# Audio tower on one core: expert heads rotated over the column tiles of TensorE, expert mixing in one 32x32 step, pooling weights moved into the stationary operand, gate logits as a product

## Chip, cores and metric

One core of a Trainium2 chip runs the whole kernel. The metric is the device time of one execution in microseconds. The kernel before takes 988.88 us (median of 3 runs, 986.07 to 990.84).

## What is computed

Every value is fp32. The reference, cut to what matters here:

```
h = tok(x, w, b)                       # x: 128 batches x 64 features x 750 times
h = h + attn(layernorm(h), Q, K, VO)
h = h + ffn(layernorm(h), ...)         # h: 128 batches x 94 tokens x 64 features

tok:    windows of 8 times; scores = x.w + b; weights = softmax over the 8;
        pooled = sum(x * weights)      # -> 94 tokens
attn:   8 heads of rank 32; softmax(q k^T / 8) over all 94 tokens; ctx = attn @ x;
        out = sum over heads of ctx @ VO
ffn:    4 heads n of width 16: sx = x @ hl_w + hl_b
        4 experts e per head: q_e = sx wq_e, k = sx wk, v = sx wv
        att = softmax(4 q k^T + causal); qkv = att v; qkv = 0 where sx == 0
        gs = softmax over e of (gate_w . qkv + gate_b); mixed = sum_e qkv_e gs_e
        hn = layernorm(mixed + resid); two 16x16 layers with relu; layernorm -> fout
        fg = softmax over the 4 heads of fout @ fgate_w^T
        out = fout * fg
```

## The kernel before

Four batches make a **quad**; there are 32. Tokens are padded to 96 and cut into three blocks of 32, called j = 0, 1, 2; nearly every tile has the 128 partitions (batch b, token within the block), with j, head and expert in the free dimension. A quad passes through some ten stages: scores of the pooling softmax (`tok_score`), transposes of x (`turn`), pooling (`pool_x`), first layer norm, attention (`project`, `score`, `exp_s`, `norm_p`, `turn_p`, `mix`, `give_outT`, `give_out`), second layer norm, the experts' projections (`front_...`), their scores (`score3`), softmax (`soft` on VectorE, the exponential on ScalarE in `exp_p3` after a transpose `turn_p3`), mixing with v (`mix3`), the mask (`guard`), the transpose back with the gate's product (`turn_c`), the gate, a norm, two small layers (`layer1`, `layer2`), a norm, the head gate and the store.

The whole is a software pipeline written out by hand. Each engine has a function `quad` that is run once per iteration and lists the steps in a fixed order, each for a different quad (`g - 3`, `g - 4`, ...); an iteration of the loop does one whole quad's worth of each step. The engines run their lists strictly in order and wait for each other by semaphores. The eight PSUM banks are shared by fixed numbers that stand in the calls, so a step on TensorE also waits until VectorE or ScalarE has emptied its bank. No scheduler is at work: the lists and the bank numbers are the schedule.

Three kinds of fact about the code matter below.

- A matmul occupies a **tile** of the 128x128 array: contraction rows x columns of its stationary operand, in multiples of 32. The profile prints it in front of the shape, as `64*32`. Matmuls on different tiles of one shape may run side by side. An fp32 matmul is executed as two passes, so the profile counts two instructions for one of the code; transposes are one each.
- `mix3` works in three shapes: `96*32` for token block 2 (L793), `32*32` for block 0 (L797, head n on rows 32n and columns 32n, so four of the sixteen tiles are used), `64*32` for block 1 (L801). To bring v onto the partitions that this needs, SyncE's queue copies it with four DMAs per quad (`move_v`).
- `scale_x` multiplies x in PSUM by the softmax weights of the pooling on VectorE, four instructions per quad (L1348, L1353); `pool_x` then sums with a constant 0/1 matrix `pick` as the stationary operand. The head gate is a product of `fo` with the broadcast `wfg` on GpSimd (L529) and a sum on VectorE (L1517).

## Time and profile before

| | |
|---|---|
| time, median of 3 runs | 988.88 us (986.07 to 990.84) |
| the profiled execution | 985.96 us, span 984.0 us |
| TensorE busy | 903.5 us, 92% |
| VectorE busy | 815.4 us, 83% |
| ScalarE busy | 732.6 us, 74% |
| GpSimd busy | 719.0 us, 73% |
| TensorE clock, mean over the span | 0.967 of full |
| DMA moved | 36.48 MB, mean 37 GB/s |

Read it as an average over three parts: a filling part in which only the first stages have work, some 28 iterations that all look alike, and an emptying part. Only windows inside the middle part tell what an iteration costs.

### The profile page before, as it was taken

To read this page: it belongs to the slowest core of one execution; us is meant where nothing else is said; L and a number is where in the kernel's file an instruction comes from. 1 tells how busy PE (TensorE), PEld (TensorE's weight loads), DVE (VectorE), ACT (ScalarE), POOL (GpSimd) and SP (SyncE) were. 2 spreads that over 40 slices of the span, in tenths; PEclk is the share of its full clock that TensorE was granted. 3 is DMA by queue.
4 is the path that set the end of the run, shared out by engine and by line. 5 is a ranking of instruction groups with operands and counts; after the bars stand their busy time and mean duration, and the time that the engine had idled before them with its cause. 6 is when DMAs were issued, how large, how long until landed. Compare 5 with 4: busy or idle time off the path is not lost.

```text
span 984.0 us, 39626 instructions
## 1 busy us (share of the span) xinstructions
PE 903.5 (92%) x16320; PEld 604.0 (61%) x16320; DVE 815.4 (83%) x1916; ACT 732.6 (74%) x2759; POOL 719.0 (73%) x1055
## 2 busy tenths in 40 slices
PE   4798999999999999999999999999999999989841
PEld 3365666666666666666666666666666666656630
DVE  3545687889898888989899888989899888889877
ACT  1566878878888888878878888878888888885520
POOL 2333245577888787888888787878889788879893
PEclk9778999999999999999999999999999999999975
DMA  6301111110111011111111011111100000000000
GB/s 199 105 7 35 42 42 41 41 42 10 45 45 36 15 43 45 45 45 45 45 45 42 11 43 44 44 46 45 45 14 14 7 13 11 14 13 15 17 8 17
DMA packets 40931, 36.48 MB, mean 37 GB/s; under 512 B 27312, under 2 KB 30512, under 8 KB 40752
## 3 DMA queue, kind: packets, MB, share of 16 engines
q1 hardware_dynamic: 40406, 33.91, 12.3%
q8 instruction: 129, 2.11, 0.9%
q14 instruction: 50, 0.41, 0.1%
q10 hardware_dynamic: 250, 0.05, 0.0%
q0 software_dynamic: 96, 0.00, 0.0%
HBM read 25.08 MB, written 3.08 MB: 29 GB/s over the span
## 4 chain that ended last, share of the span: by engine, by line
PE 75%; ACT 16%; DVE 6%; issue 1%; DMA 1%; POOL 1%; POOLq 0%; DVEq 0%
ACT pu L1123 14%; PE psum L782 10%; PE psum L808 9%; PE psum L703 7%; PE psum L731 6%; PE psum L693 5%; PE psum L685 5%; PE psum L767 5%; PE psum L610 4%; PE psum L635 3%; PE psum L711 3%; PE psum L801 2%; PE psum L821 2%; PE psum L797 2%; PE psum L817 2%; PE psum L621 2%
## 5 line engine op out<-in xcount | busy, mean ns | idle before, releaser
L1123 ACT ACTIVATE pu<-psum,mx 128x94 f32<-128x94 f32 x768 | 248.2, 370 | 8.0 <-DVE mx L1404 6.7
L1123 ACT ACTIVATION_READ_ACCUMULATOR pu<-psum,mx 128x1 f32 x768 | 182.2, 238 | 0.0
L474 POOL TENSOR_TENSOR pu<-pu,pr 128x752 f32<-128x752 f32 x96 | 138.6, 1446 | 34.3 <-DVE pr L1408 34.2
L1404 DVE TENSOR_REDUCE mx<-psum 128x8 f32<-128x752 f32 x96 | 90.1, 939 | 87.3 <-PE psum L693 83.1
L1166 ACT ACTIVATE pT<-psum 96x512 f32<-96x512 f32 (+1 forms) x224 | 131.1, 601 | 34.1 <-PE psum L782 29.9
L508 POOL TENSOR_TENSOR st<-st,neg_half 128x12 f32<-128x12 f32 x64 | 146.0, 2281 | 5.0
L782 PE MATMUL psum<-ident_w,pu 128*96 128x128 f32 (+1 forms) x896 | 132.1, 277 | 13.2 <-ACT pu L1123 7.4
L1433 DVE TENSOR_REDUCE mx<-psum 128x16 f32<-128x1536 f32 (+2 forms) x96 | 116.5, 1213 | 11.2 <-PE psum L767 11.2
L782 PEld LDWEIGHTS psum<-ident_w,pu 128*96 128x96 f32 (+1 forms) x896 | 99.5, 135 | 39.8 <-issue 17.2
L1436 DVE TENSOR_TENSOR pu<-psum,mx 128x1536 f32<-128x1536 f32 (+2 forms) x96 | 117.5, 1224 | 3.3
L808 PE MATMUL psum<-gx,ct 128*128 128x84 f32 x768 | 101.9, 276 | 0.0
L808 PEld LDWEIGHTS psum<-gx,ct 128*128 128x128 f32 x768 | 93.9, 193 | 12.9 <-issue 12.9
L693 PE MATMUL psum<-kp,xT 64*32 64x376 f32 x1536 | 83.4, 491 | 8.4 <-ACT pu L1123 6.4
L1412 DVE STREAM_TRANSPOSE pT<-pu 128x768 f32<-128x768 f32 x96 | 87.6, 941 | 0.0
L731 PE MATMUL psum<-x3T,aq 64*128 64x384 f32 x256 | 78.9, 522 | 0.0
L1128 ACT ACTIVATE cT<-psum 128x384 f32<-128x384 f32 x128 | 53.9, 493 | 33.5 <-PE psum L703 33.4
L1170 ACT ACTIVATE oc<-psum 128x336 f32<-128x336 f32 x96 | 43.0, 448 | 47.8 <-PE psum L808 47.8
L703 PE MATMUL psum<-pT,xn 32*64 32x384 f32 x1536 | 70.1, 489 | 0.3 <-ACT kp L1151 0.3
L1116 ACT ACTIVATE kp<-psum 128x384 f32<-128x384 f32 x128 | 59.7, 500 | 13.3 <-PE psum L685 13.3
L767 PE MATMUL psum<-kp,sxT 32*32 32x256 f32 (+2 forms) x3072 | 69.1, 389 | 0.0
L1444 DVE SCALAR_TENSOR_TENSOR ct<-sxT,psum 128x512 f32<-128x512 f32 x96 | 65.4, 681 | 4.1 <-PE psum L801 1.9
L525 POOL TENSOR_TENSOR ft<-ft,fx 128x192 f32<-128x192 f32 x29 | 17.2, 592 | 70.0 <-DVE ft L1512 70.0
(187 smaller groups left out, 2203.2 us busy)
## 6 DMA issues: line engine op xcount, KB each, us to landing
xs<-in_x SPq DMA_DIRECT2D x64, 375.0 KB, 3.7
vb<-va SPq DMA_DIRECT2D x32, 128.0 KB, 2.2
out_h<-ho SPq DMA_DIRECT2D x126, 16.0 KB, 1.4
out_h<-ho SPq DMA_DIRECT2D x126, 7.5 KB, 1.4
vc<-va SPq DMA_DIRECT2D x96, 16.0 KB, 2.2
gx<-in_L_ffn_gate_w SPq DMA_DIRECT2D x16, 0.2 KB
fc<-in_L_ffn_fc_w SPq DMA_DIRECT2D x12, 1.0 KB
fc<-in_L_ffn_fc_b SPq DMA_DIRECT2D x12, 0.1 KB
```

Of the source, the lines that this page charges most:

```text
L474: pool.tensor_tensor(p, p, bcast(pr[:, j, :, :].rearrange("p a b -> p (a b)"), 2, NTOK), ALU.mult).then_inc(at_normed, 1)
L508: pool.tensor_tensor(st[:, k, 3, :], st[:, k, 2, :], neg_half[:, 0:NJ * NH], ALU.pow).then_inc(rstd, 1)
L693: mm = pe.matmul(psum[TB * b:TB * b + TB, (low, high)[par], 0:HP * NTOK], xT[rows, p, b, TB * j:TB * j + TB], kp[rows, p, b, :, 0:NTOK], s ...
L703: mm = pe.matmul(psum[64 * par:64 * par + 64, banks[b], 0:HP * TP], xn[rows, r, ub, 0, :], pT[rows, :, par, :, ub, :], start=(ub == 0), st ...
L731: return pe.matmul(psum[:, bank, 0:NJ * 128], w[rows], x3T[rows, :, :].rearrange("p b t -> p (b t)"), start=True, stop=True)
L767: mm = pe.matmul(psum[QB * b:QB * b + QB, bank + n, 0:NE * w].rearrange("p (e u) -> p e u", e=NE), sxT[rows, p, j, QB * b:QB * b + QB], kp ...
L782: mm = pe.transpose(psum[0:rows, bank, 128 * e:128 * e + 128], src, ident)
L808: mm = pe.matmul(psum[:, bank, GC * e:GC * e + GC], ct3[:, i, 2 * (e % 2) + e // 2 if i == 1 else e, :], gx[:, e, :], start=True, stop=True)
L1123: ins = act.activation(pu[:, j, par, hp, 0:NTOK], psum[:, (low, high)[par], NTOK * hp:NTOK * hp + NTOK], ACT.Exp, bias=mx[:, j, par, hp:hp ...
L1166: act.activation(pT3[j][:, f - (0, 4, 6)[i], :, :, :].rearrange("p e b t -> p (e b t)"), psum[0:rows, bank, :], ACT.Exp).then_inc(p_copied, 1)
L1433: dve.tensor_reduce(mx3[:, i, :, :], S3(j, bank), AX.X, ALU.max).then_inc(shifted, 1)
L1436: dve.tensor_tensor(p, S3(j, bank), bcast(mx3[:, i, :, :], 3, QB * (j + 1)), ALU.subtract).then_inc(shifted, 1)
```

## The change

The tables of steps and banks are new on every engine, and these parts of the work are done in another way.

- **Expert softmax and mixing.** `score3` writes head n of batch b to column tile `(n + b) % 4` of bank b, where it was column tile b of bank n. Thereby the partitions of the probabilities, after their transpose, are the 32 keys of batch b, and v can stay where its projection puts it. `mix3` is one step: for each block k of keys, 16 matmuls on the 16 tiles `32*32`, into all query blocks j >= k at once. `move_v` with its DMAs is gone, and `turn_p3` is called 6 times instead of 7. `score3` is two steps instead of three: `score3_a` does j = 2, `score3_b` does j = 1 and 0 behind one causal product. The result is written with the expert index innermost, a stride of 4 elements in PSUM.
- **`turn_c`** uses four column tiles of 32 (16 matmuls with a strided stationary operand) instead of one of 128 (4 matmuls). **`project`, `front_pair`, `front_sv`, `mix`, `give_outT`, `give_out`** are cut into column tiles of 32 as well.
- **Pooling.** GpSimd multiplies `pick` by the weights (`weigh`, 2 instructions), `pool_x` has the product as its stationary operand (24 matmuls of 64 columns instead of 8 of 192), and x goes from PSUM to SBUF by plain copies: two on ScalarE, one on VectorE.
- **Head gate.** `fo` is transposed (`turn_fo`), copied, and multiplied by the gate's weights (`head_logits`, 8 matmuls of 12 columns); the product on GpSimd and the sum on VectorE are gone.
- **Copies.** Pairs of copies of 384 columns from PSUM become one of 768 for `kp`, `kp3` and `cT`.

The code's matmuls and transposes are 12680 in all where they were 9128.

```diff
-            def scale_x(n, f, bank):
...
-                    dve.tensor_tensor(xt[:, n % 2, f, 0:4, :, :], x_bank(bank).rearrange("p (k two f) -> p k two f", k=4, two=2),
-                                      bcast(w, 3, NFEAT), ALU.mult).then_inc(x_scaled, 1)
+            def weigh(n):
+                w = tok_pT[:, n // GQ % 2, 64 * (n % GQ):64 * (n % GQ) + 64].rearrange("p (f r) -> p f r", f=2)
+                for par in range(2):
+                    dst = wp[:, n % 2, :, 48 * par:48 * par + 16].rearrange("p (f q) c -> p f q c", f=2)
+                    ins = pool.tensor_tensor(dst, bcast(bcast(pick[:, :], 1, 6), 1, 2), bcast(w[:, :, par:par + 11:2], 3, 16), ALU.mult)
...
+            def score3_b(n3, bank):
...
+                    pe.matmul(both[:, :, :, QB:2 * QB], causA[rows, :, :].rearrange("p b t -> p (b t)"), bcast(causB[rows, :, :], 1, 2),
+                              start=True, stop=False, skip_group_check=True)
+                for j in (1, 0):
+                    for b in range(4):
+                        for n in range(NH):
+                            rows = slice(32 * n, 32 * n + 32)
+                            q = QB * ((n + b) % 4)
+                            mm = pe.matmul(S3(j, bank)[q:q + QB, b, :, :], sxT[rows, p, j, QB * b:QB * b + QB],
+                                           kp3[rows, p, :, b, 0:QB * (j + 1)], start=False, stop=True, skip_group_check=True)
...
-                        if j == 2:
-                            mm = pe.matmul(out_, va[0:TP, p, n, b, :], pT3[2][:, n, :, b, :], start=True, stop=True)
-                        elif j == 0:
...
+            def mix3(n3, bank):
+                for k in range(NJ):
+                    for b in range(4):
+                        for n in range(NH):
+                            rows = slice(QB * b, QB * b + QB)
+                            q = QB * ((n + b) % 4)
+                            s = SLOT3[k, k]
+                            mm = pe.matmul(psum[QB * n:QB * n + QB, bank + b, 128 * k:3 * 128].rearrange("p (j t e) -> p j e t", e=NE, t=QB),
+                                           vv[rows, n3 % 2, k, n, :], pT3[rows, s:s + NJ - k, :, q:q + QB],
+                                           start=(k == 0), stop=(k == NJ - 1), skip_group_check=True)
...
-                    mm = pe.matmul(psum[:, bank, GC * e:GC * e + GC], ct3[:, i, 2 * (e % 2) + e // 2 if i == 1 else e, :], gx[:, e, :], start=True, stop=True)
+                    for b in range(4):
+                        rows = slice(QB * b, QB * b + QB)
+                        mm = pe.matmul(psum[rows, bank, GC * e:GC * e + GC], ct3[:, j, rows, e], gx[:, e, :], start=True, stop=True)
...
+            def head_logits(bank):
+                for h in range(2):
+                    for c in range(4):
+                        rows = slice(QB * c, QB * c + QB)
+                        mm = pe.matmul(psum[rows, bank, 0:NJ * NH], foT[:, 128 * h + QB * c:128 * h + QB * c + QB], fgw[:, h, :],
+                                       start=(h == 0), stop=(h == 1))
...
-                    if exists(g, NQUAD):
-                        score(v % 2, 2, 5, 6)
+                if exists(g - 3, NQUAD):
+                    if g - 3 >= 6:
+                        pe.wait_ge(t_made, g - 8)
+                    pe.wait_ge(at_exped, 3 * g - 8)
+                    score(g - 3, 2, 6, at_scored)
...
-                    if exists(g - 4, NQUAD):
-                        dve.wait_ge(p_mixed, 3 * g - 10)
-                        guard(v % 2, 0, 7)
+                if exists(g - 7, NQUAD):
+                    dve.wait_ge(p_mixed, g - 6)
+                    guard(g - 7, 0, 1, c_guarded)
```

On TensorE, this is a stretch of an iteration before, in the middle part, printed without the waits. `x16` behind a shape is the number of equal instructions of the code; L793 and L801 are two of the three pieces of `mix3` (the third, L797, stands a few steps earlier), L610 is `turn`, L720 `give_out`, L762 and L767 `score3`, L679 `turn_x`, L782 `turn_p3`, L808 `turn_c`, L813 the transpose ahead of `layer1`.

```order
L693 MATMUL psum<-kp,xT 32x376 x8
L610 MATMUL psum<-ident_w,xs 128x128 x4
L793 MATMUL psum<-pT_2,va 32x4x32 x16
L720 MATMUL psum<-ident_w,oT 64x64 x6
L762 MATMUL psum<-causB,causA 128x4x32 x4
L767 MATMUL psum<-kp,sxT 32x384 x16
L679 MATMUL psum<-ident_w,xn 128x128 x3
L782 MATMUL psum<-ident_w,pu_1 128x128 x8
L808 MATMUL psum<-gx,ct 128x84 x4
L813 MATMUL psum<-ident_w,fx 128x128 x2
L801 MATMUL psum<-pT_1,va 32x2x32
```

And this is the stretch around the new `mix3` (L776) on the same engine now, with what each step waits for: L650 is `turn_x`, L766 `turn_p3`, L785 `turn_c`, L752 the causal product of `score3_b`.

```order
L776 MATMUL psum<-pT,vv 32x3x4x32 [waits s_shifted2,x_copied]
L776 MATMUL psum<-pT,vv 32x3x4x32 x15
L776 MATMUL psum<-pT,vv 32x2x4x32 x16
L776 MATMUL psum<-pT,vv 32x4x32 x16
L650 MATMUL psum<-ident_w,xn 128x128 [waits ln_done,r1_fxc]
L650 MATMUL psum<-ident_w,xn 128x128 x2
L766 MATMUL psum<-ident_w,pu_2 128x128 [waits fl_shifted]
L766 MATMUL psum<-ident_w,pu_2 128x128 x7
L785 MATMUL psum<-gx,ct 32x84 [waits c_guarded]
L785 MATMUL psum<-gx,ct 32x84 x15
L752 MATMUL psum<-causB,causA 128x8x32 [waits c_guarded,at_xT]
```

The three places of `mix3` have become one; it waits for VectorE's subtraction in block 2 of the next quad (`s_shifted2`), and the next `score3_b` waits for the three masks that empty its banks.

On VectorE, the middle of an iteration before: L1433 and L1436 are `soft` (largest value, subtraction), L1444 is `guard`, L1348 a `scale_x`, L1473 `mix_experts`.

```order
L1433 TENSOR_REDUCE mx<-psum 128x16 [waits s_scored]
L1436 TENSOR_TENSOR pu_2<-psum,mx 128x4x4x96 [waits s_shifted0]
L1476 TENSOR_REDUCE st<-ysq 128x12 [waits z_sq]
L1444 SCALAR_TENSOR_TENSOR ct<-sxT,psum 128x512 [waits p_mixed]
L1348 TENSOR_TENSOR xt<-psum,tok_pT 128x512 [waits x_filled]
L1433 TENSOR_REDUCE mx<-psum 128x16 [waits s_scored]
L1436 TENSOR_TENSOR pu_1<-psum,mx 128x1024 [waits s_shifted1]
L1473 TENSOR_REDUCE yc<-op 128x192 [waits g_mul]
```

The same engine now: L1368 and L1370 are `soft`, L1295 the copy of x, L1375 `guard`.

```order
L1368 TENSOR_REDUCE mx<-psum 128x16 [waits s_scored_a]
L1370 TENSOR_TENSOR pu_2<-psum,mx 128x4x12x32 [waits s_shifted2]
L1359 BN_STATS l_bn<-hj 128x6 [waits at_added]
L1359 BN_STATS l_bn<-hj 128x6 x2
L1362 MEMSET spot 1x1 [waits ln3_var]
L1364 BN_AGGR l_mv<-l_bn 128x2 x3
L1446 TENSOR_REDUCE fm<-psum 128x3 [waits fl_made]
L1448 TENSOR_TENSOR fl<-psum,fm 128x12 [waits fl_shifted]
L1295 COPY xt<-psum 128x2x256 [waits x_turned]
L1375 SCALAR_TENSOR_TENSOR ct<-sxT,psum 128x512 [waits p_mixed]
L1375 SCALAR_TENSOR_TENSOR ct<-sxT,psum 128x512 x2
```

The three masks stand in one piece behind one wait for `mix3`; they stood in three places, each behind its own part.

## Rows read from the trace of the kernel before

**Rows 1.** The page: the span, and busy time of each engine.

```profile
span 984.0 us, 39626 instructions
PE 903.5 (92%) x16320; PEld 604.0 (61%) x16320; DVE 815.4 (83%) x1916; ACT 732.6 (74%) x2759; POOL 719.0 (73%) x1055
```

**Rows 2.** Window: length, busy us PE, PEld, DVE, ACT, POOL; clock, DMA share, GB/s.

```profile
466.26:521.35 55.09, 54.41 (x1017) 36.29 (x1021) 49.16 (x117) 45.47 (x174) 45.60 (x67) 1.00 0.14 41
```

**Rows 3.** The chain that ended last: start us, us, what; first and last `mix`, 31 apart.

```profile
46.98 2.12 PE psum L703 x48
...
894.88 2.19 PE psum L703 x48
```

**Rows 4.** TensorE's timeline, middle part: start us, us, line, tile, shape, passes.

```profile
500.90 0.24 PE L801 MATMUL psum<-pT,va 64*32 64x64 f32 x1
...
501.68 0.66 PE L610 MATMUL psum<-ident_w,xs 128*128 128x128 f32 x4
502.34 0.23 PE L762 MATMUL psum<-causB,causA 32*128 32x128 bf16 x4
502.51 0.71 PE L767 MATMUL psum<-kp,sxT 32*32 32x256 f32 x32
503.15 1.12 PE L808 MATMUL psum<-gx,ct 128*128 128x84 f32 x8
504.11 0.60 PE L782 MATMUL psum<-ident_w,pu 128*96 128x128 f32 x4
504.55 0.49 PE L726 MATMUL psum<-ident_w,xn 128*128 128x128 f32 x3
...
506.43 0.50 PE L767 MATMUL psum<-kp,sxT 32*32 32x128 f32 x32
506.86 0.70 PE L817 MATMUL psum<-fxT,fc 128*128 128x256 f32 x2
...
517.65 0.29 PE L797 MATMUL psum<-pT,va 32*32 32x128 f32 x1
517.65 0.30 PE L797 MATMUL psum<-pT,vc 32*32 32x128 f32 x3
...
518.65 0.86 PE L693 MATMUL psum<-kp,xT 64*32 64x376 f32 x16
519.45 1.52 PE L711 MATMUL psum<-cT,vo_w 128*64 128x192 f32 x16
...
522.61 1.08 PE L793 MATMUL psum<-pT,va 96*32 96x128 f32 x32
523.62 0.56 PE L720 MATMUL psum<-ident_w,oT 64*64 64x64 f32 x12
```

**Rows 5.** VectorE's timeline in the same iteration.

```profile
498.77 1.73 DVE L1433 TENSOR_REDUCE mx<-psum 128x16 f32<-128x1536 f32 x1
500.53 1.76 DVE L1436 TENSOR_TENSOR pu<-psum,mx 128x1536 f32<-128x1536 f32 x1
...
503.06 0.68 DVE L1348 TENSOR_TENSOR xt<-psum,tok_pT 128x512 f32<-128x512 f32 x1
...
512.28 0.93 DVE L1517 TENSOR_REDUCE fl<-hm 128x12 f32<-128x768 f32 x1
...
518.79 0.69 DVE L1444 SCALAR_TENSOR_TENSOR ct<-sxT,psum 128x512 f32<-128x512 f32 x1
519.62 0.94 DVE L1404 TENSOR_REDUCE mx<-psum 128x8 f32<-128x752 f32 x1
```

**Rows 6.** The chain that ended last, one link: the eight exponentials of one `exp_s`.

```profile
518.51 2.57 ACT pu L1123 x16
```

**Rows 7.** Groups of instructions by line: busy us, mean ns of one, idle us before.

```profile
L1166 ACT ACTIVATE pT<-psum 96x512 f32<-96x512 f32 (+1 forms) x224 | 131.1, 601 | 34.1 <-PE psum L782 29.9
L529 POOL TENSOR_TENSOR hm<-fo,wfg 128x768 f32<-128x768 f32 x29 | 52.7, 1819 | 0.0
L512 POOL TENSOR_TENSOR yc<-yc,st 128x192 f32<-128x192 f32 x58 | 29.9, 516 | 2.5
```

1610 lines of the change are left out of this document (744 added, 866 removed).

## Prediction, as it was put on record

> **What bounds the kernel now.** I read the page first: TensorE is busy 903.5 of 984.0 us, more than any other engine [rows 1]. The average hides the edges, so the window comes next. The chain of work repeats itself, with the same links 55.09 us apart, which is two quads. In that window TensorE is busy 54.41 us, VectorE 49.16, ScalarE 45.47 and GpSimd 45.60, at full clock [rows 2]. Per quad: 27.54 us, of which TensorE 27.2, VectorE 24.6, ScalarE 22.7, GpSimd 22.8. TensorE waits 0.3 us per quad; it is the bound, and no other view can overrule that. The first and the last `mix` start 847.9 us apart, 31 steps [rows 3]; 136 us lie outside them, for filling and emptying. So a microsecond off an iteration is worth about 29 (some iterations at the edges are short of work already). The profiled execution took 985.96 us, 1.96 more than its span, and lies 2.9 under the median of the runs.
>
> TensorE's timeline gives the price of each step as the distance from its start to the start of the next [rows 4]. On the 16 small tiles a step of 256 columns takes 0.64 us and one of 128 takes 0.43: 1.65 ns a column and 0.22 us besides. `score` streams 376 columns in 0.80 us, of which 0.62 is columns: about 0.16 to 0.2 us are spent on ending one tile shape and starting the next. An iteration changes shape 27 times.
>
> **The change, part by part, for TensorE, per quad.**
> `mix3` now: 1.00 us in block 0 (517.65 to 518.65), 1.01 in block 2 (522.61 to 523.62), 0.78 in block 1 (500.90 to 501.68), 2.79 in all [rows 4]. Then: 384 + 256 + 128 = 768 columns one after the other on each of the 16 tiles, 768 x 1.65 + 0.22 = 1.49. Saved: 1.3. Bounds: the output has a stride of 4 elements in PSUM, which no row shows; if each column cost double, 1.27 more and nothing is saved.
> `turn_c`: 0.96 us (503.15 to 504.11), three times, 2.9; the stationary operand is loaded eight times at full width, and 84 columns are too few to hide that. Then 4 x 84 columns per column tile, 0.55 us each if loads into four narrow tiles go side by side, 1.65 in all; 0.96 each if they do not. I take 2.0. Saved: 0.9 (bounds 0 to 1.25).
> `score3`: two causal products fewer by one (0.17) and one change of shape fewer; saved 0.3. `turn_p3`: one of seven gone, 0.44 to 0.53, saved 0.5. `project`, `front_pair`, `front_sv` and two of three `score` steps now follow each other in one shape, eight neighbours: each loses its 0.16 us of change, and `pool_x` joins `turn_c`; saved 1.1. Added: `turn_fo` (two transposes, half of a 0.44 us step) and `head_logits`, small, with two changes of shape: 0.2 + 0.5 = 0.7. `mix`, `give_outT`, `give_out` and the token scores have the same columns per tile as before: nothing.
> Sum: 1.3 + 0.9 + 0.3 + 0.5 + 1.1 - 0.7 = 3.4. TensorE's work goes from 27.2 to 23.8 us.
>
> **The other engines.** VectorE: the four products of `scale_x` end (0.60 us from 503.06 to the next start at 503.66, another of 0.56, and two of half the size together 0.66: 1.8), as does the sum of L1517 (0.85) [rows 5]; one copy of 512 columns comes, at most the same 0.60. 24.6 - 1.8 - 0.85 + 0.6 = 22.5 busy. Its own short waits between chained instructions are about 1 us more, so no iteration can be under 23.5. ScalarE: one of seven exponentials gone and two copies of the same 512 columns added, each some 0.49 us of start-to-start (its busy mean is 601 ns [rows 7]); a copy for `foT` is 0.3, six merged pairs give back under 0.1 each: 22.7 + 0.5 + 0.3 - 0.5 = 23.0 busy. GpSimd: loses 1.82 us (L529) and gets two products of 192 columns at 0.52 (as L512 [rows 7]): 22.0. The DMAs of `move_v` end; they were on no chain. So four engines lie between 22 and 24 where one stood alone at 27. That is the point of this case: the work of TensorE alone would promise 3.4 us per quad, but the banks now couple engines with almost no slack.
>
> **Where TensorE must wait.** I laid the lists side by side for one iteration with the durations above; time 0 is the end of `soft` for j = 2. Five places do not close.
> (1) That `soft` itself: 1.73 + 1.76 us [rows 5] behind `score3_a`, and the new `mix3` waits for it. TensorE has two `turn`, `turn_fo`, two `turn_p3`, `head_logits`, `turn` and a transpose in between, 3.3 us with changes. Wait 0.3.
> (2) `score3_b` needs the three masks, 0.60 each and one behind the other (an L1444 takes 0.69, the next may start a little earlier). TensorE has 2.0 us to do (`turn_x`, two `turn_p3`, `turn_c`). Wait 0.1 to 0.2.
> (3) Banks 6 and 7: `score` j = 0, `least` (0.94), `exp_s` (2.57 [rows 6]), then `layer2`. ScalarE comes to this `exp_s` only after four merged copies, at 13.4; TensorE arrives at 15.7 and the exponentials end at 16.0. Wait 0.5.
> (4) `score` j = 2 in the same banks waits for `layer2` and VectorE's mask of it: two handovers and 0.3 us of work. Wait 0.6.
> (5) `give_out` waits for a copy that stands behind the second `exp_s`, 2.57 us. Wait 0.5 where no token scores lie between, that is in half the quads: 0.3.
> Sum 1.8, where it was 0.3. Handovers differ from my 0.1 to 0.15 us, and a wait in one place shortens the next; I take 1.7. Iteration: 23.8 + 1.7 = **25.5 us**, 2.04 less than 27.54. Times 29: 59 us. Filling and emptying stay. 988.9 - 59 = 930; I say **931 us**. The profiled span would be 926.
>
> **Rivals.**
> *The waits close.* As before, TensorE waits 0.3 to 0.8 us. Iteration 24.3, gain 3.2 x 29 = 93: 896 us. For it: in the kernel before, the lists fit to 1%. Against: VectorE would have to be busy 22.5 of 24.3 us, 93%, where it has 89% today. Chance 0.2.
> *VectorE sets the time.* If a copy from PSUM or the reordered `soft` output costs more than its row, 1 us is enough: VectorE is at 24.5 with its chain `soft` - masks - `soft` unbroken, and TensorE waits behind each mask. Iteration 26.7: 965 us. Chance 0.13.
> *Loads are not hidden.* If the 32 narrow loads of a `turn_c` do not go beside the running matmuls, it stays at 0.96 us and saves nothing: iteration 25.5 + 0.9 = 26.4, 957 us. For it: today's `turn_c` is bound by its loads. Against: those are four times as wide. Chance 0.05.
> *Narrow tiles do not run side by side* (the slower case). `score3` now has four row tiles writing one bank at a time, and `turn_c` depends on hidden loads. If matmuls of different row tiles took turns in a bank, `score3` would stream 768 columns four times: 3 x 1.27 = 3.8 us more, iteration 29.3, +51 us: 1040 us. It decides from 2.0 us more per quad. Against it: L797 has head n on rows 32n and columns 32n, all four in one bank. One `va` and three `vc` passes start at 517.65 together, and 32 passes are through in 1.00 us; by turns they would need 32 x 128 columns, 3.4 us [rows 4]. What stays open is sixteen tiles instead of four, the stride in PSUM (1.27) and that of the stationary operand (up to 0.9); both of the latter together would just do it. Chance 0.08.
> The Trainium skill, TensorEngine Tiling (Array Packing), Restrictions and Gotchas, says that different row tiles cannot access the same PSUM bank at the same time; by that, the time would be the 1040 of this rival. The trace disagrees, in the rows of L797.
> The Trainium skill, TensorE: Matmul & The Clock Gate, Part 3, says that a load overlaps running matmuls only where the row group differs; `turn_c`'s column tiles share all rows, and by this rule the 957 us of the rival before would come. The passes of L797 are no test of it, since each has a row group of its own.
> *No change.* The work saved reappears as waits almost to the microsecond: 0.04.
> The forecast itself, iteration 24.9 to 26.3, 908 to 950 us: 0.50.
>
> **Range and chances.** Low end: the first rival, 896, less a little for waits of 0.3: 890. High end: the second rival and the stride in PSUM alone (25.5 + 1.27 = 26.8, 968): 972. Beyond lie the slower case, the no-change case and some of the tails, 0.2 in all. A measurement of this kernel tells about 0.5% from no change. Faster: 0.50 + 0.2 + 0.13 + 0.05 = 0.88; within 0.5%: 0.04; slower: 0.08.
>
> **What the next profile must show.** `mix3` as one group of 96 passes in 1.5 us, not 2.8. Each `turn_c` under 0.75 us. A repeating distance of 51.0 us for two quads with TensorE busy 93 to 95%, VectorE 88 to 90%. Waits of TensorE on `exp_s`, on VectorE's mask of `layer2` and on `soft`. I am wrong in mechanism if TensorE's busy time per quad stays over 25.5 (then tiles or strides cost), or if GpSimd is what the others wait for: its list waits once for the first norm's statistics, which VectorE makes late, and has some 2 us of slack there.

## The result, and the profile after

The changed kernel takes 1022.08 us (median of 5 runs, 1019.81 to 1028.39) where the kernel before takes 987.05 (5 runs, 986.07 to 990.84): ratio 1.036, 95% interval 1.034 to 1.039. It is slower by 35 us; the forecast was 931 us, faster. The profiled execution of the changed kernel is the slowest of its five, 1028.39 us, so its losses add up to somewhat more than 35 us.

The page of the profile after, span and busy time of each engine, then the queue that brings instructions (queue, kind: packets, MB, share of 16 engines), which answer to [rows 1]:

```profile
span 1026.7 us, 53493 instructions
PE 875.7 (85%) x23616; PEld 602.5 (59%) x23616; DVE 754.3 (73%) x1786; ACT 741.7 (72%) x2631; POOL 693.8 (68%) x1087
...
q8 instruction: 185, 3.03, 1.2%
```

The same queue in the kernel before:

```profile
q8 instruction: 129, 2.11, 0.9%
```

Every engine but ScalarE (9 us more) is less busy than before, TensorE by 28 us, and the span is longer. So nothing has become the bound by work; TensorE stands still somewhere. Note the passes too: 23616 against 16320, and 56 more blocks of instructions of 16,384 bytes (3.03 MB in 185 packets).

The timeline of TensorE gives the first and the last `mix` (start us, us, engine, line, shape), which answer to [rows 3]; the last from the chain:

```profile
56.99 2.77 PE L676 MATMUL psum<-pT,xn 32*32 32x384 f32 x96
```

```profile
934.80 2.77 PE psum L676 x94
```

The first `mix` comes 10.0 us later than before, the 31 intervals take 877.8 us instead of 847.9 (29.9 more), and what follows the last takes 91.9 instead of 89.1 (2.8 more). Those are the 42.7 us between the two profiled spans. Part of the first term comes back at once: the first two intervals are short (24.48 and 25.18 us, where the kernel before has 26.72 and 29.14), so the third `mix` is only 3.9 us late (106.65 against 102.76). From there on the order loses 31.4 us in the 26 intervals up to the 29th `mix` (745.3 against 713.9), 4.6 us in the last three and 2.8 us behind them.

The window of two quads without a disturbance, in the columns of [rows 2]:

```profile
485.23:540.25 55.02, 51.91 (x1465) 36.27 (x1465) 45.76 (x110) 45.94 (x165) 43.72 (x68) 1.00 0.12 35
```

55.02 us, where before had 55.09. Undisturbed, the new order gains nothing. Two kinds of quads alternate in both kernels: one with the token scores (27.62 us now, 27.85 before) and one without (27.40 now, 27.23 before); the mean is 27.51 now and 27.54 before. TensorE's timeline of the first of these quads, answering to [rows 4] and [rows 6] (idle time before a step and its releaser in brackets; the mixed rows of `front_sv`, `score` and `front_pair` left out):

```profile
485.23 2.77 PE L676 MATMUL psum<-pT,xn 32*32 32x384 f32 x96 [0.28 <-ACT kp L1101]
487.93 0.69 PE L811 MATMUL psum<-fc,hxm 128*128 128x96 f32 x4
489.06 0.87 PE L665 MATMUL psum<-kp,xT 64*32 64x376 f32 x16 [0.45 <-DVE ft L1440]
489.85 1.51 PE L686 MATMUL psum<-cT,vo_w 128*32 128x192 f32 x32
...
492.39 0.54 PE L697 MATMUL psum<-ident_w,oT 64*32 64x64 f32 x24 [0.76 <-ACT oT L1083]
...
495.25 0.42 PE L790 MATMUL psum<-ident_w,fo 128*96 128x128 f32 x2 [0.28 <-ACT pu L1074]
...
497.83 2.12 PE L776 MATMUL psum<-pT,vv 32*32 32x384 f32 x96
499.88 0.55 PE L650 MATMUL psum<-ident_w,xn 128*128 128x128 f32 x3
...
501.23 0.82 PE L785 MATMUL psum<-gx,ct 128*32 128x84 f32 x32
...
502.24 1.28 PE L759 MATMUL psum<-kp,sxT 32*32 32x256 f32 x64
503.45 1.40 PE L785 MATMUL psum<-gx,ct 128*32 128x84 f32 x64
504.66 0.85 PE L606 MATMUL psum<-xt,wp 128*32 128x64 f32 x48
505.45 0.55 PE L703 MATMUL psum<-ident_w,xn 128*128 128x128 f32 x3
```

From start to start: `mix` 2.70 us (2.12 before), `mix3` 2.05 (2.79 before, 1.49 forecast), `turn_c` 0.79 and then 1.21 for two. 2.5 us of the 27.40 are waits (0.51 before `mix`, 0.52 before the scores of j = 2, 0.89 before `give_out`, 0.37 before `turn_fo`, 0.18 before `mix3`), 24.9 are work. The quad behind it, with the token scores, has 1.6 us of waits (0.51, 0.52, and 0.57 before `mix3`) and 26.0 of work. A mean quad is thus 25.5 us of work and 2.0 of waits, from start to start.

Now a quad that takes 30.66 us. The same stretch in its timeline:

```profile
321.18 2.11 PE L776 MATMUL psum<-pT,vv 32*32 32x384 f32 x96
...
324.57 0.82 PE L785 MATMUL psum<-gx,ct 128*32 128x84 f32 x32
325.36 0.29 PE L752 MATMUL psum<-causB,causA 32*128 32x256 bf16 x4
325.58 0.71 PE L759 MATMUL psum<-kp,sxT 32*32 32x256 f32 x32
328.04 0.51 PE L759 MATMUL psum<-kp,sxT 32*32 32x128 f32 x32 [1.75 <-issue]
328.49 1.40 PE L785 MATMUL psum<-gx,ct 128*32 128x84 f32 x64
329.70 0.63 PE L606 MATMUL psum<-xt,wp 128*32 128x64 f32 x32
331.68 0.43 PE L606 MATMUL psum<-xt,wp 128*32 128x64 f32 x16 [1.35 <-issue]
```

In the middle of `score3_b` TensorE stops for 1.75 us, and in the middle of `pool_x` for 1.35. No semaphore stands there; the view says "issue", it waited for nothing that the profile shows. The banks and operands are the same as in quads that don't stop. I counted: for each place where the next load or matmul of the same line, without a wait of its own, starts over 0.45 us after the one before it, its number among all of TensorE's instructions in the trace (loads, matmuls and the 303 semaphore and drain instructions between them), modulo 256 (edges of 100 us left out).

```
kernel before   none
kernel after    25 places, 30.0 us from start to start; number modulo 256: 194 in 23 of them, 102, 119
```

The instruction queue moved 185 packets of 16,384 bytes for TensorE's 47,535 instructions in the trace, and 129 for 33,225 in the kernel before: one packet for every 256 of them. So I take each place with the remainder 194 as the edge of a block. All but two of the stops lie on such an edge, from `turn_c` (L785) to `pool_x` (L606); the two, in `mix3` at 921 and 922 us, are not explained. TensorE's view of waits has the same stops, counted from the end of the work before them (us in total, times, longest):

```profile
PE psum L606 <- issue: 13.0, 13, 1.4
...
PE psum L785 <- issue: 6.7, 6, 1.6
...
PE psum L759 <- issue: 3.5, 4, 1.7
```

In the example the two edges are 3.64 us apart, the second stop included. The theory, then: **the instruction stream starves TensorE** (F). Its rival (W): the stops come of banks or operands, and the rest of the loss is work and waits.

The trace of the kernel after can already tell the two apart, because it holds the 185 packets of that queue one by one. Behind each edge one packet starts and takes 0.88 to 1.45 us. Between 100 us and 100 us before the end, TensorE passes none of 163 edges earlier than 1.19 us after the landing of the packet that began behind the edge before, and the 23 stops end 1.19 to 1.71 us after it, 1.36 in the median. (In the example the packets land at 326.61 and 330.33, and TensorE goes on at 328.04 and 331.68.) In the kernel before it never comes closer than 2.36 us, and it doesn't stop. So each block is asked for when the one before it is begun, and TensorE stands still when it has used that one up before the next is there. W can't say why the stops should keep this distance.

The stops are of two kinds. In 13 the packet began 0.97 to 1.24 us after the edge, and the block was simply used up too fast: these edges are 3.3 to 3.9 us apart. In 7 it began 2.1 to 4.7 us after the edge, with 194 to 256 packets of the loads of x in the queues before it. The other 3 lie between (1.6 to 1.7 us, no loads).

### The profile page after: what moved, and what is told of

The parts are those of the page before. It is cut to its first block, busy times and chain, and to the rows that moved or that the text cites. A ratio compares the mean times of both kernels' runs of the same rounds, so it can differ in the third digit from the quotient of the medians.

```text
span 1026.7 us, 53493 instructions
## 1 busy us (share of the span) xinstructions
PE 875.7 (85%) x23616; PEld 602.5 (59%) x23616; DVE 754.3 (73%) x1786; ACT 741.7 (72%) x2631; POOL 693.8 (68%) x1087
## 3 DMA queue, kind: packets, MB, share of 16 engines
q8 instruction: 185, 3.03, 1.2%
## 4 chain that ended last, share of the span: by engine, by line
PE 62%; ACT 17%; DVE 11%; issue 4%; SPq 4%; POOL 2%; DMA 0%; POOLq 0%
PE psum L676 8%; ACT pu L1074 8%; PE psum L776 7%; PE psum L785 6%; PE psum L766 6%; PE psum L657 4%; PE psum L759 4%; PE psum L710 4%; DVE pu L1370 4%; DVE mx L1368 4%; ACT cT L1079 3%; PE psum L665 3%; SPq L346 2%; PE psum L606 2%; ACT kp L1101 2%
## 5 line engine op out<-in xcount | busy, mean ns | idle before, releaser
L462 POOL TENSOR_TENSOR pu<-pu,pr 128x752 f32<-128x752 f32 x96 | 137.4, 1445 | 23.9 <-DVE pr L1346 23.8
L1368 DVE TENSOR_REDUCE mx<-psum 128x16 f32<-128x1536 f32 (+2 forms) x96 | 117.2, 1221 | 48.3 <-PE psum L759 30.7
L1370 DVE TENSOR_TENSOR pu<-psum,mx 128x1536 f32<-128x1536 f32 (+2 forms) x96 | 117.6, 1225 | 3.3
L665 PE MATMUL psum<-kp,xT 64*32 64x376 f32 x1536 | 103.1, 486 | 17.4 <-DVE ft L1440 11.6
L1112 ACT ACTIVATE pT<-psum 128x512 f32<-128x512 f32 x192 | 104.5, 595 | 14.4 <-PE psum L766 12.5
L766 PE MATMUL psum<-ident_w,pu 128*128 128x128 f32 x768 | 102.1, 277 | 1.0 <-ACT pu L1074 0.6
L676 PE MATMUL psum<-pT,xn 32*32 32x384 f32 x3072 | 88.5, 491 | 9.6 <-ACT kp L1101 8.6
L766 PEld LDWEIGHTS psum<-ident_w,pu 128*128 128x128 f32 x768 | 87.6, 142 | 3.9 <-ACT pu L1074 1.2
L1375 DVE SCALAR_TENSOR_TENSOR ct<-sxT,psum 128x512 f32<-128x512 f32 x96 | 60.3, 684 | 32.3 <-PE psum L776 32.3
L785 PE MATMUL psum<-gx,ct 128*32 128x84 f32 x3072 | 74.1, 242 | 8.2 <-issue 6.7
L776 PE MATMUL psum<-pT,vv 32*32 32x384 f32 (+2 forms) x3072 | 70.9, 403 | 10.9 <-DVE pu L1370 9.7
L676 PEld LDWEIGHTS psum<-pT,xn 32*32 32x32 f32 x3072 | 45.2, 103 | 52.4 <-ACT kp L1101 30.7
L785 PEld LDWEIGHTS psum<-gx,ct 128*32 128x32 f32 x3072 | 61.9, 139 | 21.8 <-issue 19.5
L1064 ACT ACTIVATE xT<-psum 128x384 f32<-128x384 f32 x32 | 15.7, 491 | 72.5 <-PE psum L650 72.4
L710 PE MATMUL psum<-x3T,aq 64*32 64x384 f32 x1024 | 65.8, 483 | 1.2 <-ACT hx L1121 1.2
```

The lines of the kernel that those rows point to most:

```text
L462: pool.tensor_tensor(p, p, bcast(pr[:, j, :, :].rearrange("p a b -> p (a b)"), 2, NTOK), ALU.mult).then_inc(done, 1)
L665: mm = pe.matmul(psum[TB * b:TB * b + TB, bank + par, 0:HP * NTOK], xT[rows, n % 2, b, TB * j:TB * j + TB], kp[rows, n % 2, b, :, 0:NTOK], ...
L676: mm = pe.matmul(psum[q:q + 32, bank + b, 0:HP * TP].rearrange("p (h j t) -> p h j t", h=HP, j=NT), xn[rows, n % 4, ub, 0, 32 * c:32 * c + ...
L710: mm = pe.matmul(psum[32 * n:32 * n + 32, bank + half, 0:NJ * 128], aq[rows, e + half, n, :], x3T[rows, :, :].rearrange("p b t -> p (b t)" ...
L766: mm = pe.transpose(psum[:, bank, 128 * e:128 * e + 128], pu3[j][:, e, k, :, :].rearrange("p b u -> p (b u)"), ident)
L776: mm = pe.matmul(psum[QB * n:QB * n + QB, bank + b, 128 * k:3 * 128].rearrange("p (j t e) -> p j e t", e=NE, t=QB), vv[rows, n3 % 2, k, n, ...
```

## The experiments

All ratios are to the kernel before, run on the same chip. "Pauses" are counted as above, from start to start (the expectations speak of 23 and 29 us, or, with the fill, of 33). "Undisturbed" are the two intervals between one `mix` and the next that repeat themselves where no pause falls, without and with the token scores. Each kernel has one profile, and executions of one kernel differ (those of the kernel after by 8.6 us), so pauses of the profiled execution and medians of the time don't subtract exactly.

```
kernel        median us  ratio (95% interval)     first mix  undisturbed    pauses
after         1022.1     1.036 (1.034 to 1.039)   56.99      27.40, 27.62   25, 30.0 us
a_turnc1      1125.0     1.141 (1.136 to 1.145)   56.81      31.14, 31.37   0
a_mix64       1017.7     1.030 (1.026 to 1.034)   55.76      26.99, 27.48   30, 28.8
a_smallload   1014.5     1.026 (1.023 to 1.030)   54.71      27.40, 27.62   12, 11.7
a_lateload    1013.6     1.027 (1.024 to 1.030)   56.27      27.40, 27.62   17, 15.9
a_movepool    1034.7     1.048 (1.046 to 1.050)   56.64      28.27, 28.49   16, 14.9
a_fill        1016.4     1.031 (1.028 to 1.035)   51.23      27.40, 27.62   25, 28.5
a_fix1        1028.4     1.042 (1.039 to 1.045)   46.08      27.88, 28.36   19, 18.1
a_swap        1021.8     1.034 (1.030 to 1.039)   57.23      27.27, 27.76   26, 29.6
a_mix3flat    1020.5     one run                  56.60      27.40, 27.62   22, 24.4
a_fix2        1001.8     1.016 (1.011 to 1.020)   48.44      26.99, 27.49   17, 15.9
f2_exp4        995.5     1.009 (1.007 to 1.011)   47.36      26.90, 27.05   20, 18.2
f2_halfpool    987.5     1.001 (0.999 to 1.003)   45.49      26.81, 27.30   8, 7.8
f2_both        982.8     0.995 (0.993 to 0.997)   49.32      26.69, 26.85   11, 11.1
b_turnc4       983.5     0.996 (0.994 to 0.997)   46.92      27.04, 27.78   3, 1.6
b_best         987.2     1.001 (0.999 to 1.002)   45.66      27.18, 27.91   0
b_mix32       1006.7     1.021 (1.019 to 1.022)   46.48      27.79, 28.43   0
```

### What the pauses are

**a_turnc1**, the stretch with 144 instructions fewer:

```
-                    for b in range(4):
-                        rows = slice(QB * b, QB * b + QB)
-                        mm = pe.matmul(psum[rows, bank, GC * e:GC * e + GC], ct3[:, j, rows, e], gx[:, e, :], ...)
+                    mm = pe.matmul(psum[:, bank, GC * e:GC * e + GC], ct3[:, j, :, e], gx[:, e, :], ...)
```

> The kernel after, with turn_c in one 128-column stationary instead of four of 32 (48 passes fewer for each quad from 96 to 24 passes, 144 load and matmul instructions fewer of about 640 in the stretch from mix3 to pool_x). Theory F (TensorE starves for instructions: they come in blocks of 256, one transfer each, and the dense stretch uses a block faster than the next one arrives): the pauses in mid-step without a semaphore, 23 of them and 29 us in the kernel after, fall to fewer than 8 and under 10 us; the instruction transfers fall from 185 to about 167; the matmul work grows by about 0.9 us a quad (29 us), so that the time lies between 1010 and 1035 us, but with full steps in place of pauses. Theory W (no starving; the pauses come of banks or operands, and the loss is work and waits of the new order): the pauses stay at 25 to 29 us and the time goes to 1045 us or more.

The pauses are gone, all of them, and 167 blocks came. But the time rose by 103 us, far over the range of F; W had 1045 us or more, with the pauses unchanged. The lines of `turn_c` in the kernel before (L808), after (L785) and here (L783): duration in ns, min/median/max.

```profile
L808 PEld LDWEIGHTS psum<-gx,ct x768: 186/192/338, 115.5 to 945.2; 128*128 128x128 f32 x192
L808 PE MATMUL psum<-gx,ct x768: 238/275/423, 115.6 to 945.3; 128*128 128x84 f32 x192
```

```profile
L785 PEld LDWEIGHTS psum<-gx,ct x3072: 134/136/173, 122.7 to 988.3; 128*32 128x32 f32 x192
```

```profile
L783 PEld LDWEIGHTS psum<-gx,ct x768: 307/330/333, 124.5 to 1091.0; 128*128 128x128 f32 x192
L783 PE MATMUL psum<-gx,ct x768: 350/397/529, 124.6 to 1091.1; 128*128 128x84 f32 x192
```

Same shape as in the kernel before, but `ct3` now has the expert as its innermost axis, so the stationary operand is read at every fourth element: 330 ns a load instead of 192, and the step takes 1.92 us, not 0.86. Three such steps in place of 2.0 us make 3.8 us a quad, and the undisturbed intervals are 3.74 longer, 116 us over 31 quads. The missing pauses take 30 off, and nine intervals of 32.6 to 33.0 us, which were not looked into, add most of the rest. In 32 columns the same stride is nearly free (136 ns; 110 in b_turnc4, where it is contiguous). So the narrow tiles of `turn_c` are what makes the new layout bearable. Slower steps also use instructions more slowly; the vanished pauses agree with F but do not prove it alone.

**a_smallload** and **a_lateload**, the same TensorE program with the x loads changed:

```
-                    load(g + 6)
+                    for p in (2 * g + 12, 2 * g + 13):
+                        sp.dma_start(xs[0:16, p % NSLOT, 0:NTIME], x_pairs[p][0:16]).then_inc(x_loaded[p % NSLOT], 16)
```

```
                     sp.wait_ge(x_turned, 3 * g + 3)
+                    if g >= 1:
+                        sp.wait_ge(at_proj, 2 * g)
                     load(g + 6)
```

> The kernel after, but of the x loads behind the first 12 pairs only 16 of the 128 partitions are moved (so the later quads are computed from old data). Theory F with the loads as part of it (an instruction transfer waits in the DMA queues behind the 256 packets of 3,000 bytes of a quad's load): pauses fall from 29 us to 10 to 18 us, time 1004 to 1012 us. F without it (the transfer's own round trip of about 3.6 us is what counts): pauses stay over 22 us, time 1016 to 1024 us. Theory W: 1019 to 1025 us, pauses unchanged.

> The kernel after, where SyncE issues the x loads of a quad behind the two project steps instead of at the start of the iteration, so that their 256 packets of 3,000 bytes don't lie in the queues during the stretch from turn_c to pool_x. Nothing is left out; a load has four iterations until it is read. Theory F with the loads as part of it: like the kernel with small loads, pauses from 33 us to 15 to 20 us, time 1008 to 1014 us. F with the loads no part: pauses and time as after, 1020 to 1025 us. A rival (the loads reach their readers too late): a new wait of tok_score for the loads, over 1025 us.

Not one instruction of TensorE differs, and the pauses fall from 30.0 to 11.7 and 15.9 us, the time by 8 to 10 us. The line of `pool_x` in the same view of a_smallload, where it was 13.0:

```profile
PE psum L607 <- issue: 8.6, 13, 1.2
```

That decides for F against W, and with the loads as part of it: an instruction block that is fetched while the 256 packets of 3,000 bytes are in the queues comes later. The packets agree: in a_smallload those of the 12 stops left all began 0.59 to 1.06 us after the edge before, and none of the late ones is left. Every pause left in these two kernels lies at number 194 modulo 256. In the profiled executions, which are 20.6 and 12.6 us faster than that of the kernel after, the 18.3 and 14.1 us of pauses are nearly the whole difference. The median of a_smallload missed its range (1004 to 1012) by 2.5 us.

**a_movepool**: `pool_x(g - 2, 5)` moved behind `front_turn` and `turn_p3(2)`, its waits left where they were.

> The kernel after, with the 24 matmuls of pool_x (96 load and matmul instructions) issued behind front_turn and the second turn_p3, seven long transposes later, instead of right behind the two turn_c; its waits stay where they were. Same instructions, same banks, same 185 instruction transfers. Theory F (TensorE starves in a stretch that uses 100 instructions a microsecond, with one block of 256 per 3.6 us arriving): the pauses, 29 us in the kernel after, fall to under 18 us, the time to 1005 to 1014 us. Theory W (the loss is in work and waits alone): no change, 1019 to 1025 us.

The pauses halve, to 14.9 us, as F has it; and the time rises by 12 us, since something else was moved. The timeline:

```profile
508.47 0.88 PE L606 MATMUL psum<-xt,wp 128*32 128x64 f32 x48
509.89 0.63 PE L766 MATMUL psum<-ident_w,pu 128*128 128x128 f32 x4 [0.54 <-ACT hj L1040]
```

`turn_p3(5)` writes the bank of `pool_x` and now stands right behind it, so it waits for ScalarE's copy of `hj`: 0.64 us more in each quad. The undisturbed intervals are 0.87 longer in all, 27 us over 31 quads; less the 15 us of pauses, that is the 12 us that the time rose. I had counted the instructions and not the bank.

### What the longer fill is

**a_fill**: `split_w`, `make_w` and `copy_m` one iteration later.

```
-                if g - 4 == 0:
+                if g - 5 == 0:
                     split_w()
```

> The kernel after, with split_w, make_w and copy_m one iteration later, so that VectorE and TensorE don't stop for the last of the small weight transfers (landed at 46 us) ahead of the first attention scores. Theory 1 (the fill is longer because the new order puts this wait ahead of quad 0's scores): the first mix comes 4 to 6 us earlier than 56.99 us, the time is 1015 to 1019 us. Theory 2 (the fill is longer because the software pipeline is deeper): no change in the first mix, 1020 to 1025 us.

The first `mix` starts at 51.23 instead of 56.99, and the time falls by 5 to 6 us, as theory 1 has it. But the 5.8 us at the first `mix` are not what reaches the end: the third starts at 104.95 instead of 106.65, 1.7 us earlier, and the rest of the gain lies in the later intervals, 1.5 us of it in the pauses. In the kernel after, the chain of the first 60 us ran through the issue of the small weight loads by SyncE and the landing of the last of them:

```profile
40.69 0.43 issue
41.12 4.85 DMA bet<-in_L_ffn_fnorm_b
46.56 0.33 DVE whl L1301
```

The remaining 4 us at the first `mix` were not followed further. They are not firm: in a_fix1, with the same edit, the first `mix` starts at 46.08, earlier than in the kernel before.

### What narrow tiles cost and give

**a_mix64** and **b_mix32**, `mix` back to 32x64 tiles in the new kernel, and cut to 32x32 in the old one:

```
-                        for c in range(2):
-                            for b in range(4):
-                                q = 64 * par + 32 * c
-                                mm = pe.matmul(psum[q:q + 32, bank + b, ...], xn[rows, n % 4, ub, 0, 32 * c:32 * c + 32], ...)
+                                q = 64 * par
+                                mm = pe.matmul(psum[q:q + 64, bank + b, ...], xn[rows, n % 4, ub, 0, :], ...)
```

> The kernel after, with mix in 32x64 tiles as in the kernel before (24 matmuls instead of 48). In the profile after, mix took 2.69 us for 96 passes, against 2.12 us for 48 in the kernel before. Both theories: mix back to about 2.1 us, 0.57 us less for each quad, 18 us over 31 quads if nothing takes its place, a time of 1004 to 1010 us. F: the pauses in the dense stretch stay within a third of their number (mix is not in it), only at other places, since the block boundaries move. If the prediction's view was right (mix costs nothing more in narrow tiles), the time stays at 1022 us.

> The kernel before, with its mix alone cut into 32x32 tiles (48 matmuls instead of 24). The prediction priced this at nothing. By the profile after, 96 passes take 2.69 us against 2.12 us for 48: 0.57 us a quad more, 1000 to 1006 us. If narrow tiles cost nothing in this order: 985 to 990 us.

In the kernel before, the narrow tiles alone cost 20 us (1006.7, at the upper end of the range). The rows, b_mix32 and then a_mix64:

```profile
497.08 2.77 PE L705 MATMUL psum<-pT,xn 32*32 32x384 f32 x96
```

```profile
501.15 2.20 PE L675 MATMUL psum<-pT,xn 32*64 32x384 f32 x48 [0.28 <-ACT kp L1100]
503.72 0.69 PE L810 MATMUL psum<-fc,hxm 128*128 128x96 f32 x4 [0.36 <-ACT pu L1073]
```

The same columns for each tile, 0.57 us apart. (Both edits also change in which order batches and column tiles follow each other; that alone was not run.) In the new kernel only 6 of 18 us come back, outside both ranges: `layer2`, behind `mix`, now has to wait 0.36 us for the exponentials, and the mean undisturbed interval falls by 0.27 and not by 0.57.

**b_turnc4** (`turn_c` alone in four tiles, in the kernel before) and **b_best** (`project`, `give_outT` and `give_out` as well):

> The kernel before, with turn_c alone cut into four 32-column tiles (12 matmuls become 48, 144 instructions more for each quad). The prediction's term: turn_c from 2.9 to 2.0 us a quad, so up to 28 us less, 960 to 965 us, if nothing else keeps the time. Theory F: the same saving of work, and no pauses to speak of, since here the three turn_c lie apart; 129 instruction transfers become about 147; 960 to 972 us. A rival (the cut itself costs: narrow tiles do not run side by side or their loads are not hidden): 1000 us or more.

> The kernel before, with turn_c, project, give_outT and give_out cut to 32 columns and its mix kept in 32x64 tiles: the narrow tiles without the new order. turn_c alone gave 4.9 us. From the profile after, against before: project 1.31 against 1.58 for the pair, give_outT 1.38 against 1.45, give_out 0.47 against 0.50 us, together 0.37 us a quad, 12 us if all of it is on the path: 972 to 978 us. If the waits of the order before take it up: 980 to 985 us.

b_turnc4 is the fastest that computes everything: 0.4% under the kernel before. But 4.9 us is a sixth of the expected 28. Its timeline, to be read beside [rows 4]:

```profile
504.55 0.80 PE L810 MATMUL psum<-gx,ct 128*32 128x84 f32 x32
505.28 0.64 PE L782 MATMUL psum<-ident_w,pu 128*96 128x128 f32 x4
505.76 0.49 PE L726 MATMUL psum<-ident_w,xn 128*128 128x128 f32 x3
506.18 0.79 PE L810 MATMUL psum<-gx,ct 128*32 128x84 f32 x32
506.90 0.64 PE L782 MATMUL psum<-ident_w,pu 128*96 128x128 f32 x4
507.58 0.24 PE L762 MATMUL psum<-causB,causA 32*128 32x128 bf16 x4
```

The first `turn_c` lasts 0.73 us to the next start, where it was 0.96; but the transposes behind it take 0.48 and 0.42 instead of 0.44 and 0.33. From this `turn_c` to the causal product two steps behind the next one it is 3.03 us against 3.11 (503.15 to 506.26). What a narrow step gains, the wide step behind it gives back in large part: the three `turn_c` of a quad are 0.50 us shorter together, the steps behind them 0.33 longer, and the mean undisturbed interval falls by 0.13. b_best, with three more kinds of steps narrow, gives nothing and misses both of its ranges; its interval is 27.55 in the mean, 0.14 over that of b_turnc4. Why is open.

**a_mix3flat**: `mix3` writes `"p (j e t) -> p j e t"` instead of `"p (j t e) -> p j e t"`.

> The kernel after, with mix3 writing each expert's 32 outputs side by side in its bank instead of every fourth element (the readers are left as they are, so they read the values in another order). The prediction had 1.49 us for the 96 passes of mix3, the profile shows 2.04 us. If the stride of the write costs it: 1.5 to 1.7 us. If it is the load of the instructions and weights of 96 small passes: 2.0 us again.

```profile
493.20 2.12 PE L776 MATMUL psum<-pT,vv 32*32 32x384 f32 x96
```

To the hundredth what it was, 2.05 us from start to start. The stride of the output costs nothing. What does is seen beside the prediction's price, 1.65 ns a column and 0.22 us a step: `mix3` lies 0.56 us over it with 96 passes, `mix` in 32x32 tiles 0.58 with 96, `score3_b` 0.36 with 64, and `score3_a` not at all with 32. The excess goes with the number of passes; no run varied that number alone within `mix3`.

### What the waits are

**a_swap**: `front_pair(2, 2)` ahead of the scores of j = 0 instead of behind them.

> The kernel after, with front_pair(2) issued ahead of the scores of j=0 instead of behind them, so that ScalarE's copy for it is done before mix wants its banks (mix waits 0.5 us for it in the profile after). Theory A (the waits are separate, each can be taken away): mix's wait goes, 0.4 to 0.5 us a quad, 1007 to 1012 us. Theory B (the iteration is held by one circle, scores, exponentials and masks through bank 6): the scores come 0.64 us later, layer2 waits that much longer for the exponentials, and the time stays or rises, 1020 to 1030 us.

```profile
510.84 2.77 PE L676 MATMUL psum<-pT,xn 32*32 32x384 f32 x96
514.03 0.69 PE L811 MATMUL psum<-fc,hxm 128*128 128x96 f32 x4 [0.42 <-ACT pu L1075]
```

The wait ahead of `mix` is gone and stands ahead of `layer2`, 0.49 us long (510.84 to 514.03 is 3.19, the step 2.70). The quads without token scores are 0.13 us shorter and those with them 0.14 longer; the mean, 27.52, is what it was. The time is what theory B forecast.

**a_fix1** (mix64, fill, movepool) and **a_fix2** (mix64, fill, lateload):

> The three edits together: mix in 32x64 tiles, pool_x behind the transposes, split_w and make_w one iteration later. If they add up: minus 6 (mix, measured), minus 10 to 16 (F), minus 4 to 6 (fill), 994 to 1004 us. If the waits of the new order take up what the steps give: 1005 to 1012 us. Under 985 us (faster than the kernel before) neither theory gives.

> The kernel after with mix in 32x64 tiles, split_w and make_w one iteration later, and the x loads behind project. If the three add up (minus 6, minus 5, and minus 8 to 14 for the loads by theory F): 997 to 1003 us. If the order's waits take them up: 1005 us or more. Neither gives less than the kernel before.

a_fix1 lies far outside both ranges: it carries the 0.87 us a quad of a_movepool with it (its intervals are 0.87 and 0.89 longer than those of a_fix2), and its pauses, 18.1 us, are not fewer than without that edit. In a_fix2 the three parts add up, 20 us together, and it is still 15 us behind the kernel before.

**f2_exp4, f2_halfpool, f2_both**, a_fix2 with work left out:

```
-                    for hp in range(HP):
+                    for hp in range(2 if j == 0 and n >= 4 else HP):
```

```
-                    for par in range(2):
+                    for par in range(1):
```

> The version with mix in 32x64 tiles, the later split_w and the later x loads (1001.8 us), in which ScalarE computes only 4 of the 8 exponentials of j=0 from the fifth quad on (the rest of the weights are left from the quad before, so the output differs). Theory B (each iteration is held by the circle scores j=0, exponentials, layer2, mask, scores j=2 in bank 6): 1.28 us less in the circle, the waits in front of layer2 and of the scores of j=2 shrink by 0.4 to 0.9 us together, the undisturbed iteration falls from 27.0 to 26.1 to 26.6 us, the time to 975 to 990 us. Theory C (TensorE's own work or VectorE's queue holds it): 27.0 us stay, 998 to 1004 us.

> The same version (1001.8 us), with pool_x cut to 12 of its 24 matmuls (half of the pooling sum is left out, so the output differs): 48 load and matmul instructions fewer behind the turn_c. Work alone gives 0.39 us a quad, 12 us: 989 to 991 us, pauses as they were (22 us). Theory F (a stretch dense in instructions starves): the pauses fall to under 12 us as well, time 975 to 985 us.

> Both edits. If the pauses and the circle are what keeps the new order from its gain: 950 to 970 us. If not, 985 us or more.

f2_exp4 speaks against my circle through bank 6 as what holds every quad. Four exponentials fewer take the wait ahead of `layer2` away,

```profile
485.72 2.19 PE L677 MATMUL psum<-pT,xn 32*64 32x384 f32 x48 [0.28 <-ACT kp L1103]
487.85 0.69 PE L812 MATMUL psum<-fc,hxm 128*128 128x96 f32 x4
488.98 0.87 PE L667 MATMUL psum<-kp,xT 64*32 64x376 f32 x16 [0.45 <-DVE ft L1443]
```

and the undisturbed intervals go from 26.99 and 27.49 to 26.90 and 27.05 only, 0.26 in the mean of the 1.28 us that were taken out. The time, 995.5, lies between the ranges of the two theories. In TensorE's waits between 300 and 850 us (us in total, times, longest), a_fix2 and then f2_exp4, it is seen where they went:

```profile
PE psum L812 <- ACT pu L1076: 7.3, 20, 0.4
PE psum L698 <- ACT oT L1085: 5.6, 11, 0.7
```

```profile
PE psum L698 <- ACT oT L1085: 8.6, 10, 1.1
```

7.3 us went, 3.0 came back ahead of `give_out`. f2_halfpool takes 24 passes out of the dense stretch. Its median is 14 us lower; in the profiled executions, 22 us apart, the pauses make 8 (15.9 to 7.8) and the undisturbed intervals, 0.18 us shorter where 0.39 us of work went, make 6; 3 are an earlier first `mix`, and the rest was not located. The pauses fell as F has it, the time missed the range of F by 2.5 us. f2_both takes another 5 us off and ends between its two ranges. What sets the 26.7 to 27.0 us in the end is not settled: no single wait does, for each one that was removed came back elsewhere for the most part. Even without most pauses, most of the fill's loss and some real work, the new order is where the old one was.

## Why the prediction was wrong

**What bounds the kernel**: right. TensorE was the bound before, and it is the engine that loses the time now.

**TensorE's work, 23.8 us a quad**: this is the step that failed first. It was too low by 1.7; 25.5 was measured for a mean quad (24.9 without the token scores, 26.0 with them). Mis-sized: `mix` in narrow tiles was priced at nothing and costs 0.57 (b_mix32: 20 us by itself); `mix3`, 1.49 forecast, takes 2.05, because I priced it by columns, and the passes cost as well (a_mix3flat clears the stride, my bound of 1.27); `score3` saved nothing instead of 0.3 (0.16 + 0.86 + 0.22 + 1.21 = 2.45 against three times 0.81 in the mean before); `turn_c` came out at 2.0 as forecast, but from 2.7 and not 2.9. Those are 1.6 of the 1.7. In the other direction, the six `turn_p3` (0.97 or 0.87 a pair) save about 0.7, not 0.5. The rest, among it the 1.1 us for changes of shape, was not taken apart.

**Waits, 1.7 us**: 2.0 in the mean quad. The four that were named are there: `soft` 0.38 in the mean (forecast 0.3), the mask of `layer2` 0.52 (0.6), `give_out` 0.89 in every second quad (0.3 in the mean); the masks ahead of `score3_b` and the exponentials ahead of `layer2` cost nothing, until a_mix64 or a_swap moved the wait there. (For the exponentials the prediction has 0.5, where its own times, 15.7 and 16.0, give 0.3.) Not named: 0.51 ahead of `mix` for ScalarE's copy of `kp3`, and 0.37 ahead of `turn_fo` in every second quad. That the sum came out near is in part luck: these two stand in for the two that didn't come. The two terms, 1.7 and 0.3, take the whole 2.0 us of gain: 27.5 instead of 25.5 forecast and 27.5 before. By busy time, the measure from which the forecast set out (27.2 and 0.3), it is 25.96 and 1.56, since the ends of the matmuls reach into the waits; the miss is then all in the work. "No change", which I gave 0.04, is what the undisturbed iteration does. The forecasts for the other engines were good: VectorE 22.9 us busy (22.5), ScalarE 23.0 (23.0), GpSimd 21.9 (22.0).

**"Filling and emptying stay"**: failed, and smaller than it looks. The first `mix` is 10 us late, 5.8 of them shown by a_fill to be the wait for the last small weight load, which the new order has ahead of the first scores; by the third `mix` 3.9 us are left. The last three intervals lose 4.6 us and the end 2.8.

**Not in the prediction at all**: the supply of instructions. 23616 passes are 47232 loads and matmuls, 45% more than before, and 424 of them stand in 4.2 us from `turn_c` to `pool_x`. The pauses are 30 us in the profiled execution, and 27.5 of them stand in the 26 intervals that lose 31.4 us against the kernel before. I counted columns, loads, banks and waits of each step, and took for granted that the steps can be issued. It is this that turns no change into 3.6% slower, with the fill and the end.

**The rivals.** "Narrow tiles do not run side by side", the slower one, had the right sign and the wrong mechanism: the 64 passes of `score3_b`, each of whose banks gets output from four row tiles, take 1.21 us, and by turns they would take over twice that. The Trainium skill, TensorEngine Tiling (Array Packing), Restrictions and Gotchas, which excludes different row tiles in one bank at a time, is again not what the trace shows. "Loads are not hidden": 32 loads of 136 ns would be 4.35 us one after the other, and `turn_c` is through in 0.6 to 0.8 although its four tiles share all rows. The Trainium skill, TensorE: Matmul & The Clock Gate, Part 3, has loads overlap only where the row group differs; this trace disagrees, with those numbers. "VectorE sets the time": it is busy 22.9 us of 27.5; no.

**The signs that I named.** `mix3` in 1.5 us: no. `turn_c` under 0.75: 0.79, then 0.60. 51.0 us for two quads: 55.0. TensorE busy 93 to 95%: it is 94% of the undisturbed window, but of a longer one. I had written that I would be wrong in mechanism if TensorE's busy time per quad stayed over 25.5: it is 25.96. That sign was right.

## What to carry to other kernels

Cutting a matmul into narrower tiles multiplies its instructions, and they have to be fetched: where several such steps stand one behind another, count the loads and matmuls per microsecond, look at the instruction queue in the profile, and look for stops marked "issue" in mid-step; if the trace holds the packets of the queue, see whether the stops end at one distance from their landing. Price a step of small passes by the passes as well as by the columns, and a narrow step together with the wide one behind it. And when the trace before shows one engine busy and the others at 83 to 89%, a saving on that engine is worth what the next waits leave of it: here 6 of 18 us in a_mix64, 5 of 28 in b_turnc4, nothing clear of noise of 15 in a_swap.

## What the runs showed of the hardware

- TensorE's instructions arrive in blocks of 16,384 bytes, 256 instructions (185 packets for 47,535 instructions). At about 100 loads and matmuls a microsecond (424 in 4.2 us) TensorE outruns them and stops for 0.5 to 2.1 us, nearly always at the same remainder of 256. Where the packet isn't held up, two edges of blocks with a stop at the second lie 3.3 to 3.9 us apart, pause included: about 1 us to the start of the packet, about 1 us for it, and 1.36 us from its landing to the next instruction. Behind the packets of a load of x it began 2.1 to 4.7 us after the edge. Less traffic in the DMA queues at that time halves the pauses (30.0 to 11.7 or 15.9 us).
- Reading a 128-column stationary operand at every fourth float takes 330 ns instead of 192, and the whole step 1.92 us instead of 0.86 to 0.96; with 32 columns it is 136 against 110 ns.
- An output with a stride of four floats in PSUM costs `mix3` nothing: 2.05 us either way.
- 96 passes of 32x32 tiles take 2.69 us where 48 passes of 32x64 with the same columns take 2.12.
- A step of wide tiles behind a step of narrow ones takes longer than behind a wide one: three transposes 0.42 us instead of 0.33, four 0.48 instead of 0.44 (b_turnc4 against the kernel before).
